# Step one of a graph kernel: three places for transposed blocks, products two chunks behind, two accumulators, one pair of banks for logits

## What is computed

```
def _top_p_attention(X, W1, W2, W3):
    q = X @ W1.T @ W2.T
    k = X @ W3.T
    probs = softmax(q @ k.T, axis=-1)
    # keep the largest entries of each row until their sum reaches 0.9
    ...
    return A / max(A.sum(-1), 1e-12)
R = adj + eye(N);  R = R / R.sum(-1)
Z = 0;  Xf = x;  Xa = x
for n in range(2):
    A = _top_p_attention(Xa, W1, W2, W3)
    Xf = R @ Xf
    Xa = A @ Xa
    Z = Z + Xf @ U1[n].T + Xa @ U2[n].T
out = layernorm(x + layernorm(x + Z) * ln_g + ln_b)
```

## Time and profile before

| what | us |
|---|---|
| median of 3 runs (1642.64 to 1643.18) | 1642.84 |
| the profiled execution, its own time | 1643.45 |
| its span, first to last instruction | 1641.7 |
| PE busy | 1243.3 (76%) |
| DVE busy | 1411.7 (86%) |
| ACT busy | 893.5 (54%) |
| POOL busy | 173.0 (11%) |

### The profile page before, as it was taken

The page is one execution under the profiler, slowest core; times in us unless marked ns, Lnnn a source line. Parts: engine busy times, 40 slices in busy tenths (PEclk is TensorE's granted clock), DMA queues, the critical chain, the costliest instruction groups (busy, mean ns, idle before and its releaser), DMA issues.

```text
span 1641.7 us, 29435 instructions
## 1 busy us (share of the span) xinstructions
PE 1243.3 (76%) x9162; PEld 1058.4 (64%) x9162; DVE 1411.7 (86%) x7395; ACT 893.5 (54%) x1685; POOL 173.0 (11%) x357
## 2 busy tenths in 40 slices
PE   8888888888888989898988957539672909366870
PEld 4666765667676978787877856537562808365870
DVE  4788878888885989898899988989898989988984
ACT  5676667766666555555566543515552525335435
POOL 0200000000010331322212100001000100000000
PEclk9999999999999989898989988869785959778885
DMA  5100000000021431222305130303030211203101
GB/s 178 43 2 1 2 1 2 2 1 2 2 82 45 152 141 63 106 92 78 132 37 168 43 125 1 126 1 125 2 126 1 85 42 43 84 1 126 43 1 42
DMA packets 16588, 96.40 MB, mean 59 GB/s; under 512 B 1251, under 2 KB 8930, under 8 KB 9730
## 3 DMA queue, kind: packets, MB, share of 16 engines
q1 hardware_dynamic: 16384, 94.14, 16.3%
HBM read 92.43 MB, written 1.70 MB: 57 GB/s over the span
## 4 chain that ended last, share of the span: by engine, by line
DVE 68%; PE 17%; issue 7%; ACT 5%; DVEq 1%; DMA 0%; SPq 0%; ACTq 0%
DVE cand L745 18%; DVE junkC L788 17%; PE bank L546 8%; DVE E L1119 6%; DVE E L1121 6%; PE bank L525 3%; PE bank L486 3%; DVE slots L843 2%; ACT E L620 2%; DVE sub L944 2%; DVE junkS L788 2%; DVE st L796 1%; DVE st L797 1%; DVE st L798 1%; DVEq L924 1%
## 5 line engine op out<-in xcount | busy, mean ns | idle before, releaser
L647 ACT ACTIVATE blkT<-bank 128x512 f32<-128x512 f32 (+1 forms) x728 | 411.9, 566 | 500.2 <-PE bank L525 496.0
L745 DVE MAX8 cand<-E 128x8 f32<-128x32 f32 (+1 forms) x3172 | 409.7, 187 | 16.3 <-ACT E L597 15.5
L546 PEld LDWEIGHTS bank<-X,blkT 128*128 128x128 f32 x2704 | 337.0, 195 | 132.6 <-issue 67.3
L546 PE MATMUL bank<-X,blkT 128*128 128x128 f32 (+1 forms) x2704 | 380.9, 284 | 48.7 <-ACT blkT L647 47.5
L525 PE MATMUL bank<-ident,E 128*128 128x128 f32 x1144 | 196.0, 300 | 281.3 <-DVE E L1121 281.3
L525 PEld LDWEIGHTS bank<-ident,E 128*128 128x128 f32 x1144 | 153.6, 157 | 286.0 <-DVE E L1121 284.6
L788 DVE SCALAR_TENSOR_TENSOR junkC<-cand,st 128x208 f32<-128x208 f32 (+1 forms) x416 | 301.9, 762 | 3.7
L525 PE MATMUL bank<-ident,S 128*128 128x128 f32 x1560 | 240.5, 274 | 7.0 <-DVE S L1121 6.1
L486 PE MATMUL bank<-kT,Q 64*128 64x512 f32 (+1 forms) x728 | 196.7, 615 | 7.8 <-ACT E L597 6.9
L546 PE MATMUL bank<-YA,blkT 128*128 128x128 f32 x1352 | 194.0, 289 | 1.1 <-ACT blkT L647 1.1
L597 ACT ACTIVATE E<-bank 128x512 f32<-128x512 f32 (+1 forms) x308 | 157.8, 565 | 64.8 <-PE bank L486 64.0
(11 more groups left out here) (203 smaller groups left out, 1159.3 us busy)
## 6 DMA issues: line engine op xcount, KB each, us to landing
S<-in_adj_dram SPq DMA_DIRECT2D x50, 1663.5 KB, 6.9
S<-in_adj_dram SPq DMA_DIRECT2D x2, 1455.6 KB, 8.2
X<-in_x_dram SPq DMA_DIRECT2D x6, 256.0 KB, 4.1
out_dram<-H SPq DMA_DIRECT2D x2, 768.0 KB
S<-in_adj_dram SPq DMA_DIRECT2D x2, 194.9 KB, 9.5
u_in<-in_L_gnn_U_dram SPq DMA_DIRECT2D x4, 64.0 KB, 9.5
w_in<-in_L_gnn_W_dram SPq DMA_DIRECT2D x2, 32.0 KB, 2.1
X<-in_x_dram SPq DMA_DIRECT2D x1, 64.0 KB
```

The lines of the kernel that those rows point to most:

```text
L546: m = pe.matmul(bank[int(u.acc)][:, 0:width], blkT[:, slot, b * P:(b + 1) * P], rhs[:, j, 0:width], start=(j == 0), stop=(j == NT - 1))
L647: act.activation(blkT[:, slot, 0:w], BLK[early][slot][:, 0:w], ACT.Copy).then_inc(blk_done, 1)
L745: v.max(cand[:, par, xx, 8 * r:8 * r + 8], E[where_e[self.s, self.p]][:, xx, r * w:min((r + 1) * w, N)]).then_inc(s_max, 1)
```

## The change

Step one is set up as step two is:

- `RING` = 3 places of `blkT` and three banks (2, 4, 5) for turned blocks everywhere.
- `look` is 2 everywhere: `multiply` comes two chunks behind `turn`.
- The accumulator is bank 3 or 6 by turns, everywhere.
- The logits have banks 0 and 1 alone (`LG`). The two matmuls for chunk c now each wait until ACT has stored the logits of chunk c - 1 of the same row tile (`before = q - 1`); before, they waited for chunk c - 2. Banks 6 and 7 are still used for the logits of pair 0.
- The wait of the first body of step two for all earlier logits goes.

No instruction of work is added or removed.

```diff
-        u.ring, u.accs = (2, ("6",)) if b.early else (3, ("3", "6"))
-        u.acc = u.accs[u.k % len(u.accs)]
+        u.acc = ("3", "6")[u.k % 2]
-            slot = len(b.seqs) % u.ring
+            slot = len(b.seqs) % RING
-        b.look = 1 if early else 2
+        b.look = 2
...
-        LG = [[[bank[0], bank[1]], [bank[2], bank[3]]], [[bank[0], bank[1]]]]
-        BLK = {True: [bank[4], bank[5]], False: [bank[2], bank[4], bank[5]]}
+        LG = [bank[0], bank[1]]
+        BLK = [bank[2], bank[4], bank[5]]
...
-            if q < NCH:
-                return FIRST_LG
-            ring = LG[0] if q < late_logits else LG[1]
-            return ring[q % len(ring)]
+            return FIRST_LG if q < NCH else LG
...
-                before = q - (1 if q < NCH or q >= late_logits else 2)
-                if q in (NCH, NCH + 1):
-                    before = NCH - 1
+                before = q - 1
...
-                if not b.early and b.p < 0:
-                    pe.wait_ge(logits_done, 2 * late_logits)
```

More of the change, by code:

```diff
@@ L60, in gnn_top_p_kernel @@
     assert START_R + TURN_R + sum(STEP_R) == 2 * NT
+    RING = 3
     class Unit:
@@ L322, in lg_seq @@
             return (s * NPAIR + p) * NCH + c
-        late_logits = NPAIR * NCH + EARLY[1]
         def lg_banks(q):
-            if q < NCH:
-                return FIRST_LG
-            ring = LG[0] if q < late_logits else LG[1]
-            return ring[q % len(ring)]
+            return FIRST_LG if q < NCH else LG
         @block.sync
@@ L511, in _, with turn @@
             pe.wait_ge(setup_done, 13)
-            def turn(g, early):
+            def turn(g):
                 u, c, slot = seq_unit[g], seq_chunk[g], seq_slot[g]
@@ L524, in turn @@
                     j = c * CH + b
-                    m = pe.transpose(BLK[early][slot][:, b * P:(b + 1) * P], src[:, j * P:(j + 1) * P], ident[:, :])
+                    m = pe.transpose(BLK[slot][:, b * P:(b + 1) * P], src[:, j * P:(j + 1) * P], ident[:, :])
                 m.then_inc(blk_ready, 1)
@@ L575, in _ @@
                     if 0 <= i - b.off < len(b.seqs):
-                        turn(b.seqs[i - b.off], b.early)
+                        turn(b.seqs[i - b.off])
                     if i in b.emit:
@@ L639, in exponentials, with empty_block @@
                         ins.then_inc(e_ready, 1)
-            def empty_block(g, early):
+            def empty_block(g):
                 slot = seq_slot[g]
@@ L646, in empty_block @@
                     act.wait_ge(blk_used, seq_before[g] + 1)
-                act.activation(blkT[:, slot, 0:w], BLK[early][slot][:, 0:w], ACT.Copy).then_inc(blk_done, 1)
+                act.activation(blkT[:, slot, 0:w], BLK[slot][:, 0:w], ACT.Copy).then_inc(blk_done, 1)
             def store_sums(u):
@@ L693, in _ @@
                     if 0 <= i - b.off < len(b.seqs):
-                        empty_block(b.seqs[i - b.off], b.early)
+                        empty_block(b.seqs[i - b.off])
                     if i in b.emit:
```

## The result

The changed kernel takes 1673.45 us (median of 4 runs, 1672.67 to 1674.69) against 1642.74 us for the kernel before on the same chip: a ratio of 1.019, with a 95% interval of 1.0172 to 1.0208. It is slower by 30.7 us, where 18 were forecast, and 1.5 us above the range. The way and the place were right, the size was not: one term of the sum, the clock, was put at +2 us and is some +14 to +16.

The account below looks back on a forecast made before the run. A loop of PE and ACT in step one was taken to bound the kernel. 14.2 - 0.4 + 2.3 + 2 = +18.1 us on the profiled 1643.45 us, with the median 0.6 us lower, gave 1661 us; range 1651 to 1672.

Parts of the forecast that it names:

- the clock: PE after its pauses in step one: longer pauses, low stretch a little longer, +2 us, with ends -16 and +16 us.
- The loop of PE and ACT: Step one: this loop sets the 34.2 us period; rival that DVE's slack hides the loss, time stays 1643, chance 0.04.
- A single pair of banks: Bodies of p = 0 to 10: PE restarts 0.46 us later and 1.06 us of chunk 1's logits come behind it.
- The product two chunks behind: Step one, PE under the exponentials: gains nothing, since the logits of chunk 1 stand ahead of chunk 2's turning and block.
- Two accumulators: Where a body's second unit begins: PE's wait for the copy of the first unit's sums goes, 0.23 us.
- The first body: Exponentials of pair 0 after ACT's step 1: later restart and work moved behind it, less shorter waits for sums, +2.3 us.
- the waits and work: Step one without the clock: 14.2 us for bodies p = 0 to 10, -0.4 for p = 11 and 12, +2.3 first body.
- The clock costs more: Rival: with the longer pause the low stretch doubles, +16 instead of +2, 1675 us; chance of ending over 1672: 0.10.
- Within a pair's body the new order costs nothing else: Steady part of a body: the new wait for logits stores costs nothing; step two takes the same time, shifted.

Follow-up runs that it names:

- one_pair_two_acc: The kernel before with banks 0 and 1 only for step one's logits and two accumulators everywhere; look 1 and two places stay: 1678.5 us.
- before_late: The kernel before, where the first product of the bodies of p = 0 to 10 also waits for both stores of chunk 0's logits: 1661.4 us.
- restart_logits: The kernel before with 2 idle matmuls in the form of the logits between the copy of block 0 and the product of chunk 0: 1682.0 us.
- restart_products: The kernel before with 5 idle products between the copy of block 0 and the product of chunk 0, bodies of p = 0 to 10: 1660.5 us.

## Why the prediction was wrong, point by point

*The loop of PE and ACT sets the period, and DVE hides nothing.* Right. DVE's waits grew from 33.8 to 61.1 us while the loss was paid in full.

*A single pair of banks: restart 0.46 us later, 1.06 us of logits behind it.* Right in kind. The restart came 1.11 us behind the copy's start, against 0.72 before (253.08 - 252.36), so 0.39 us later. With the low clock away on both sides a period costs 1.45 us more, against a forecast of 1.29.

*The product two chunks behind gains nothing.* Too low: `look` 2 with three places gave back about 5 us between one_pair_two_acc and the changed kernel.

*Two accumulators: 0.23 us a body.* The wait went, as these rows of the changed kernel show that answer to the first two of the earlier trace rows; the product follows the turning by 0.43 us, not 0.67:

```profile
250.78 0.60 PE L519 MATMUL bank<-ident,E 128*128 128x128 f32 x4
251.21 1.06 PE L540 MATMUL bank<-X,blkT 128*128 128x128 f32 x8
```

*The first body: +2.3 us.* The distance from the first search to the second grew by 3.2 us (40.22 against 37.05), with a longer low stretch in it.

*The clock: +2 us, with ends at -16 and +16.* This is the step that failed. PE's work at the low clock went from 39.5 to 72.4 us, which by the half is 16.4 us of time, the upper end of my own bounds. The periods without a low stretch give it another way: of the 2.65 us by which a period grew, 1.45 stand at the high clock, so 1.20 are the clock's, 13.2 us in 11 periods, where the half gives 15.1. So the term is some 14 to 16 us with the first body, and the waits and work, forecast at 16.1 (14.2 - 0.4 + 2.3), are the other 15 to 17 of the 31.4 us up to the first search of step two.

I had the rows for a warning and read them wrongly. That pauses of up to 6.8 us were cheap I took from the constant period of the kernel before. But the one pause of that length ends behind the last of the 11 periods, so their length says nothing of it, and its low stretch, 454.0 to 460.8 us, is twice as long as the others, though only 3.0 us of it are work:

```profile
457.80 2.05 PE L546 MATMUL bank<-X,blkT 128*128 128x128 f32 x8 [6.80 <-ACT blkT L647]
```

Inside the 11 periods no pause passed 4.9 us, and all restarts were on products. The pause itself was forecast at over 4 us and came to 5.6 to 6.3. What I left out is a second pause ahead of it, in which PE waited for DVE's masking in seven of the 11 bodies:

```profile
247.08 0.65 PE L525 MATMUL bank<-ident,S 128*128 128x128 f32 x4 [2.08 <-DVE S L1121]
```

In the changed kernel this wait is gone from all of them: PE's body had grown and the masking was done in time. PE turns and makes logits 2 us sooner, and those 2 us join the pause under the exponentials. The change made the pause longer and put logits first behind it, and the runs show that each of these adds work at the low clock: before_late the one (39.5 to 58.2 us), restart_logits against restart_products the other (81.2 against 55.7). The rival "the clock costs more", 1675 us, came within 2 us of the result and had 0.10. The range was also narrower than I said: by my own chances it left out up to 0.25, not fewer than 2 in 10.

The page of the Trainium skill that I weighed ("TensorE: Matmul & The Clock Gate", section "HAM oscillation — how this bites in real kernels") pays the return to the high clock once for each pause. Here a pause did not have one price: the work at the low clock per low stretch was 39.5 / 12 = 3.3 us before (the 13th pause had none) and 72.4 / 13 = 5.6 us after.

*Within a pair's body the new order costs nothing else, and step two is unchanged.* Right: 1116.3 us from step two's first search to the end, against 1118.3.

## What to carry to other kernels

When a change makes PE stand still longer, or changes what it does first behind a pause, price the clock apart from the waits: here it was nearly half of the loss, and one microsecond more of pause cost nearly two. Where a loop of several engines waits for a long step of one of them, a ring of buffers is worth what it lets PE do under that step; two banks taken from the logits for a third place of blocks moved 1.06 us per pair from under the cover to behind it. If PE must wait anyway, idle matmuls that nobody waits for can be worth more than any order of the real ones (1633.1 us against 1641.7).

## What the runs showed of the hardware

- After pauses of 3.5 to 4.8 us PE was back at the high clock 2.9 to 5.4 us behind a restart with 128-row products, and 5.9 to 9.3 us behind one with 64-row matmuls 512 columns wide. Two such matmuls, one into each of two banks, took 1.06 us at the high clock and 2.48 us, more than twice as long, at the low one.
- 40 idle transposes (4.53 us) in the pause kept the clock up as well as 20 idle products (4.63 us): 1649.6 and 1649.4 us.
- Partly filled pauses are no use: 10 products or 20 transposes, which left 4.0 and 4.1 us, gave 1680.7 and 1680.6 us, 7 us above the kernel with no filling at all. Those idle matmuls shortened the pause from about 6 us and the time at the low clock from 112.6 to 85.3 and 81.9 us, but moved it from the pause onto PE's work: 83.5 and 79.8 us of it, instead of 72.4. Why the low stretch begins where it does is not shown; it speaks against a simple rule of "the shorter the pause, the better".
